# The input blocks of a scan kernel: four transfers of two blocks become two transfers of three

## What is computed

```python
def step(prev, x_i):
    y = jnp.einsum('oc,nch->noh', Wc, prev) + conv_b[None, :, None]
    y = jnp.where(y >= 0, y, prelu_a * y)
    cur = y + x_i
    return (cur, cur)

x = jnp.moveaxis(feature, 3, 0)          # feature is the group-normalised x
_, fwd_rest = jax.lax.scan(step, x[0], x[1:])
fl = jnp.concatenate([x[0:1], fwd_rest], axis=0)
_, bwd_rest = jax.lax.scan(step, fl[-1], fl[:-1], reverse=True)
out = jnp.concatenate([bwd_rest, fl[-1:]], axis=0)
# result: x + moveaxis(out, 0, 3)
```

## Time and profile before

| what | before |
|---|---|
| median of 3 runs | 376.21 us (376.13 to 376.4) |
| the profiled execution | 376.23 us |
| its span | 374.5 us |
| TensorE busy, matmul | 351.1 us (94%) |
| VectorE busy | 287.5 us (77%) |
| ScalarE busy | 230.1 us (61%) |
| GpSimd busy | 17.3 us (5%) |

### The profile page before, as it was taken

The page is one execution under the profiler, slowest core; times in us unless marked ns, Lnnn a source line. Parts: engine busy times, 40 slices in busy tenths (PEclk is TensorE's granted clock), DMA queues, the critical chain, the costliest instruction groups (busy, mean ns, idle before and its releaser), DMA issues.

```text
span 374.5 us, 10099 instructions
## 1 busy us (share of the span) xinstructions
PE 351.1 (94%) x3100; PEld 349.8 (93%) x3100; DVE 287.5 (77%) x925; ACT 230.1 (61%) x810; POOL 17.3 (5%) x30
## 2 busy tenths in 40 slices
PE   0269999999999999999999999999999999999996
PEld 0169999999999999999999999999999999999996
DVE  2688899788887887665666878778778787787786
ACT  4776656656556566565565665656656656566564
POOL 2078000000000000000000000000000000000000
PEclk9999999999999999999999999999999999999999
DMA  8997000000000000000000121212212212122122
GB/s 326 425 416 292 2 0 1 0 0 0 1 0 0 1 0 0 0 0 0 0 0 0 59 83 57 84 64 76 84 56 84 78 62 84 58 82 84 56 112 84
DMA packets 10232, 26.30 MB, mean 70 GB/s; under 512 B 1264, under 2 KB 1520, under 8 KB 9712
## 3 DMA queue, kind: packets, MB, share of 16 engines
q1 hardware_dynamic: 10224, 26.22, 18.0%
HBM read 13.63 MB, written 12.58 MB: 70 GB/s over the span
## 4 chain that ended last, share of the span: by engine, by line
PE 91%; DMA 6%; SPq 1%; DVE 1%; ACT 1%; issue 0%; ACTq 0%
PE psum L369 88%; DMA xin<-in_x 6%; SPq L247 1%; PE psum L327 1%; PE psum L317 1%; DVE state L547 0%; DVE state L553 0%; ACT state L399 0%; ACT state L393 0%; PE psum L290 0%; PE psum L286 0%; PE psum L279 0%; ACT below L462 0%; PE psum L302 0%; ACT dev L410 0%
## 5 line engine op out<-in xcount | busy, mean ns | idle before, releaser
L369 PE MATMUL psum<-state,w_t 128*128 (+1 forms) x2976 | 332.6, 275 | 0.0
L369 PEld LDWEIGHTS psum<-state,w_t 128*128 128x128 f32 x2976 | 332.4, 192 | 0.1
L462 ACT ACTIVATE below<-psum,negative 128x128 f32<-128x128 f32 x376 | 139.7, 372 | 129.3 <-PE psum L369 128.4
L547 DVE SCALAR_TENSOR_TENSOR state<-below,negative,state 128x128 f32 (+1 forms) x376 | 130.8, 348 | 64.9 <-ACT below L462 56.6
L464 ACT ACTIVATE above<-psum,params 128x128 f32<-128x128 f32 x376 | 140.0, 372 | 0.0
L553 DVE TENSOR_TENSOR state<-above,state 128x128 f32 (+1 forms) x376 | 100.7, 288 | 6.5
L599 DVE TENSOR_TENSOR state<-state,xin (+1 forms) x45 | 31.1, 692 | 0.0
L474 DVE BATCH_NORM_STATS2 bstat<-xin 128x6 f32<-128x512 f32 x32 | 20.3, 676 | 11.2 <-DMA xin<-in_x 11.2
L492 DVE TENSOR_SCALAR state<-xin,mean,rstd 128x320 f32<-128x320 f32 (+2 forms) x72 | 27.9, 434 | 0.0
L279 PE MATMUL psum<-chan,centre 128*128 128x64 f32 (+1 forms) x8 | 2.1, 361 | 17.1 <-DVE chan L488 17.1
L279 PEld LDWEIGHTS psum<-chan,centre 128*128 128x128 f32 x8 | 1.6, 250 | 17.4 <-issue 13.9
(11 more groups left out here) (38 smaller groups left out, 27.7 us busy)
## 6 DMA issues: line engine op xcount, KB each, us to landing
out_y<-state SPq DMA_DIRECT2D x47, 256.0 KB, 2.0
xin<-in_x SPq DMA_DIRECT2D x4, 1536.0 KB, 13.8
xin<-in_x SPq DMA_DIRECT2D x5, 768.0 KB, 19.6
xin<-in_x SPq DMA_DIRECT2D x7, 256.0 KB, 18.6
w_t<-in_w SPq DMA_DIRECT2D x4, 256.0 KB, 9.9
xin<-in_x SPq DMA_DIRECT2D x1, 512.0 KB, 23.4
out_y<-state SPq DMA_DIRECT2D x1, 192.0 KB, 1.9
out_y<-state SPq DMA_DIRECT2D x1, 64.0 KB, 1.6
```

Source lines behind the costliest of these rows:

```text
L369: mm = nc.tensor.matmul(psum[:, 4 * par + o, 0:COLS], w_t[:, k, o * P:(o + 1) * P], xs[k], start=k == 0, stop=k == 3)
L462: nc.scalar.activation(below[:, par, o, :], z, ACT.Relu, bias=negative[:, o:o + 1], scale=-1.0).then_inc(below_done, 1)
L547: nc.vector.scalar_tensor_tensor(sts[o], below[:, par, o, :], negative[:, KT:KT + 1], sts[o], ALU.mult, ALU.add).then_inc(part_done, 1)
```

## The change

`PAIRS` is replaced by `RUNS`: blocks 1 to 3 are one transfer, blocks 4 to 6 are one transfer, and each has rows of 18432 bytes a partition where the pairs had 12288. Blocks 7, 8 and 9 have a transfer each, as blocks 0, 10, 11 and 12 have in both kernels; the pieces of 13 to 15 are the same. All blocks of a run share the semaphore of its first block. Since a run now crosses no fixed border of a tile in the destination, `xin` is addressed by block alone, and the host lays x out to match. Nothing else is changed.

```diff
-PAIRS = {2: 3, 4: 5, 6: 7, 8: 9}
+RUNS = {1: 3, 4: 6}
+
+IN_RUN = {b: first for first, last in RUNS.items() for b in range(first + 1, last + 1)}
...
-def transfers(blocks, per_tile, steps):
+def transfers(blocks, steps):
 
     found = []
-    for b in (b for b in range(blocks) if b not in PAIRS.values()):
-        n0, n1, w0 = b % per_tile, (PAIRS[b] if b in PAIRS else b) % per_tile + 1, 0
+    for b in (b for b in range(blocks) if b not in IN_RUN):
+        w0 = 0
         for i, size in enumerate(PIECES.get(b, [steps])):
-            found.append((b, i, b // per_tile, n0, n1, w0, w0 + size))
+            found.append((b, RUNS.get(b, b) + 1, i, w0, w0 + size))
             w0 += size
     return found
...
-        for first, second in PAIRS.items():
-            x_loaded[second] = x_loaded[first]
+        for b, first in IN_RUN.items():
+            x_loaded[b] = x_loaded[first]
...
-            for b, i, k, n0, n1, w0, w1 in transfers(NBLK, N, W):
-                end = begin + P * (n1 - n0) * (w1 - w0) * H
-                sp.dma_start(xin[:, k, n0:n1, w0:w1, :],
-                             x[begin:end].rearrange("(p n w h) -> p n w h", p=P, n=n1 - n0, w=w1 - w0)).then_inc(
+            blocks = xin[:, :, :, :, :].rearrange("p k n w h -> p (k n) w h")
+            for b, b1, i, w0, w1 in transfers(NBLK, W):
+                end = begin + P * (b1 - b) * (w1 - w0) * H
+                sp.dma_start(blocks[:, b:b1, w0:w1, :],
+                             x[begin:end].rearrange("(p b w h) -> p b w h", p=P, b=b1 - b, w=w1 - w0)).then_inc(
                                  x_loaded[b][i], 16)
```

More of the change, by code:

```diff
@@ L694 @@
     slope = np.broadcast_to(np.asarray(inputs["L0_conv_prelu_a"]).reshape(1, 1), (P, 1))
-    tiles = x.reshape(N, KT, P, H, W).transpose(1, 2, 0, 4, 3)
+    blocks = x.reshape(N, KT, P, H, W).transpose(2, 1, 0, 4, 3).reshape(P, KT * N, W, H)
     arrays = {
-        "in_x": np.concatenate([tiles[k, :, n0:n1, w0:w1, :].ravel() for _, _, k, n0, n1, w0, w1 in transfers(KT * N, N, W)]),
+        "in_x": np.concatenate([blocks[:, b:b1, w0:w1, :].ravel() for b, b1, _, w0, w1 in transfers(KT * N, W)]),
         "in_w": taps[:, :, 0, taps.shape[3] // 2].T,
```

## The result

| what | before | after |
|---|---|---|
| median of 12 runs each | 376.18 us (376.13 to 376.40) | 377.19 us (376.81 to 377.30) |
| the profiled execution | 376.23 us | 377.18 us |
| its span | 374.5 us | 375.3 us |
| the scan's first L369/L372 matmul | 38.75 us | 39.57 us |

The ratio is 1.0024, with a 95% interval of 1.0017 to 1.0031: the change costs 1.0 us by the medians and 0.9 by the ratio. The two profiled executions are 0.95 apart. In their spans 0.8 is seen, all of it ahead of the scan: from its first matmul to the end of the span it is 335.75 us before and 335.73 after. The other 0.15 lies outside the two spans. The lines of the changed kernel are three higher: L369 is L372, L290 is L293, L317 is L320.

The account below looks back on a forecast made before the run. The scan's matmuls are 88% of the span; its start is set by TensorE, VectorE and GpSimd meeting. Stream 0, statistics 1.0, scan 0: 376.2 + 1.0 = 377.2 us, range 376.4 to 377.6.

Parts of the forecast that it names:

- The stream is no longer: DMA load of x: up to block 12, transfers take 24.18 us against 24.19 before, counted as zero change.
- The 0.1 that the prediction drew from it: DMA load: by the 1 MiB rule, single blocks 7 to 9 would be some 0.1 us slower together.
- ScalarE in lockstep: ScalarE: block 4 starts 1.84 us late, at 16.50; block 6 waits for its round trip to TensorE, until 20.13.
- One sign: VectorE: expected to be idle for long up to 10.9 and again up to 16.4.
- The twelve slow passes: TensorE: keep_up(9, 0), 2.79 us ahead of tile 1's group variances, puts L290 at 26.5 and GpSimd's power at 27.5.
- GpSimd's 0.48: GpSimd: idle time before its last power absorbs about 0.5 of 1.5 us, leaving that power 1.0 late.
- The second way: VectorE and TensorE: block 10's statistics wait for ScalarE, L279 goes to 33.8, 1.1 late; some 0.2 won back, 0.9 left.
- The first: Rival on TensorE: it becomes fast before keep_up(9, 0) is through, absorbing lateness; 376.3 to 376.9, chances 0.24 and 0.09 by form.
- half form: TensorE turns fast during keep_up(9, 0): L290 at 26.0, GpSimd 0.9 late, 0.4 at the end, 376.6; chance 0.24.
- full form: TensorE turns fast before 24.0: L290 near 25.2, GpSimd's 0.5 lateness swallowed, 376.3 to 376.4; chance 0.09.
- The long rows as a gain: Rival on the DMA load: long rows flow faster, at most 0.16 us gained, 376.1; chance 0.02.
- the late triples as a loss: Rival on the DMA load: triples charged as singles, everything behind 16.45 is 0.3 later, 377.5; chance 0.05 with other waits.

Follow-up runs that it names:

- fast passes: Changed kernel with 72 more TensorE passes ahead of tile 0's group deviations, 16 and 24 around its group variances: 376.29 us, ratio 1.000.
- the second triple alone: Against the kernel before, only blocks 4 to 6 in one three-block transfer; blocks 1 and 7 alone, 2-3 and 8-9 paired: 377.25 us, ratio 1.0028.

## Why the prediction was right

The number is no luck: on the way over GpSimd, which ends last, the terms behind it held too, once the landing of x is allowed for. The first block is begun at 5.25 in the profiled execution of the changed kernel and later in that of the kernel before:

```profile
5.45 0.69 DVE L474 BATCH_NORM_STATS2 bstat<-xin 128x6 f32<-128x512 f32 x1 [5.45 <-DMA xin<-in_x]
```

This 0.20 isn't the change's doing, as the kernels with untouched transfers have 5.23 to 5.31 in the profiles of the experiments. Counted from there, block 4 on ScalarE is 1.83 late (forecast 1.84), the variances of tile 1 are 1.79 late (1.73), the second power 1.53 (1.5), and the scan 1.02 (1.0). In the spans each is 0.20 less, and that is how 0.8 is seen there.

*The stream is no longer.* Right. VectorE's first instruction of block 1 is at 10.72 and that of block 4 at 16.23, 5.51 apart, where the straight line said 5.49. In the changed kernel VectorE no longer waits for the last piece, but with fast passes it does so again:

```profile
32.91 1.38 DVE L480 BATCH_NORM_STATS2 bstat<-xin 128x6 f32<-128x512 f32 x2 [0.39 <-DMA xin<-in_x]
```

That is 27.56 behind its block 0, at 5.35; in the kernel before it was 27.53 (5.45 to 32.98). The Trainium skill, page "DMA: Bandwidth & Descriptors", section "Rules for kernel authors", wants at least 1 MiB per transfer. The 0.1 that the prediction drew from it isn't seen in these 0.03; as the same interval is 27.48 to 27.65 in four other kernels' profiles, it isn't refuted either.

*ScalarE in lockstep.* Right: block 6 was put at 20.13 and came at 19.91, its early arrival is of no use, and its channel statistics wait 0.99 for ScalarE. One sign was wrong beside it: VectorE was to be idle for long up to block 4, and is idle for 1.02.

*The twelve slow passes.* Right. L290 was put at 26.5 and came at 26.36; the power on GpSimd at 27.5 and came at 27.27. The experiments show the slow pace to be the cause: with all of TensorE fast the changed kernel loses nothing, and with twelve passes more the old kernel loses as well. How much the twelve alone would give back, with the group products left slow, no run shows.

*GpSimd's 0.48.* Right: no idle time is left there, and 1.33 less 0.48 is the 0.8 by which the scan starts late in the two spans. *The second way*, by VectorE and TensorE, was priced too high: the deviations of tile 3, L279 at 32.65, were put at 33.8 and came at 33.37, 0.7 late and not 1.1. Of the 0.4 between them 0.2 is the landing again (block 10's channel statistics at 28.48, not 28.7). The other 0.2 VectorE makes up, which from there to block 14's channel statistics takes 4.62 (to 33.10) in place of 4.83 (27.54 to 32.37).

*The rivals.* The first, TensorE fast in time, was priced rightly. Its half form is in the profile of the second triple alone: the variances at 26.15 (26.0 was put), the second power 0.92 late (0.9), and 376.72 or 0.45 lost (0.4). Its full form is the kernel with fast passes, 376.29 (376.3 to 376.4). Of the 12 executions of the changed kernel itself none is in the full form and one, 376.81, in the range of the half form, so that the chance of 0.33 looks too high. The Trainium skill, page "TensorE: Matmul & The Clock Gate", Part 1, has the moment of the step change from run to run. The two groups of the kernels with 12 and 20 more passes, 1.0 us apart, fit that, but no execution of a lower group was profiled. The long rows as a gain, and the late triples as a loss, have no part in it.

## What to carry to other kernels

A transfer of several blocks hands over its first block with its last, and what that costs isn't seen in the stream, which stays full, but in the engine that takes the blocks in order and has a round trip to another engine between them. Look for work that is free only because the thing behind it is waiting anyway, such as passes that keep an engine busy: when the input comes later, it stands on the path in full. A lateness is paid only beyond the least slack of the engines behind it (here 0.48 us), so follow it to each of them before you price it.

## What was not expected

TensorE was slow up to 26.7 although it had been at work from 15.7 with pauses of no more than 0.70, in the profiled execution of the changed kernel with 20 more passes. The granted clock column reads 1.00 in both kinds of stretch, so only the durations of a pass (421 and 275 ns) tell the two levels, 1.2 and 2.4 GHz, apart. With 72 passes in one piece it was fast in the profile by 15.8 and stayed so over pauses of 0.85 and 0.40. What divides the two cases was not tried further. Keeping it fast from the start makes the two kernels alike, at medians of 376.29 and 376.28, but neither faster than the kernel before: VectorE then waits for the last piece of x in both, 0.39 and 0.40 us, as it did there.
